# Post-norm Mamba-like block with FP4 feed-forward: skip, silus, copies and g product moved up, scales interleaved, loop written out

## The reference

```
xp, z  = split(x @ W_in)                           # W_in 256 x 1024
xc     = silu(causal conv over time(xp, 4 taps) + conv_b)
ssm    = xc @ W_xproj                              # 33 columns: delta, B (16), C (16)
delta  = softplus(ssm[..., 0])
h_mean = einsum(xc, delta * B) / L                 # one 512 x 16 state per batch
y      = (einsum(h_mean, C) + D * xc) * silu(z)
x      = layernorm(x + y @ W_out)
gate, up = fq(x) @ fq(w_gate).T, fq(x) @ fq(w_up).T   # 704 columns each
h      = silu(gate) * up
x      = layernorm(x + fq(h) @ fq(w_down).T)
```

## Time and profile before

| | before |
|---|---|
| median of 3 timed runs | 2334.24 us (2331.59 to 2337.22) |
| profiled execution | 2339.92 us, span 2338.1 us |
| mean granted clock of TensorE | 0.959 |
| busy: PE, PEld, DVE, ACT, POOL | 2050.8, 1615.6, 1701.5, 1279.5, 988.0 us |
| DMA | 191.35 MB, mean 82 GB/s |

### The profile page before, as it was taken

The page is one execution under the profiler, slowest core; times in us unless marked ns, Lnnn a source line. Parts: engine busy times, 40 slices in busy tenths (PEclk is TensorE's granted clock), DMA queues, the critical chain, the costliest instruction groups (busy, mean ns, idle before and its releaser), DMA issues.

```text
span 2338.1 us, 38729 instructions
## 1 busy us (share of the span) xinstructions
PE 2050.8 (88%) x10532; PEld 1615.6 (69%) x10532; DVE 1701.5 (73%) x3292; ACT 1279.5 (55%) x2612; POOL 988.0 (42%) x1643
## 2 busy tenths in 40 slices
PE   2887799999899998999999999899989999888886
PEld 1555577777777777777777777777767777666665
DVE  6223477877787777777777787878778877777775
ACT  2556555655555656555655565555555655433343
POOL 2222344444444444444444444444444444434342
PEclk9879999999999999999999999999999999888898
DMA  2223322222222222222222222222222222111100
GB/s 74 86 72 113 111 93 95 84 86 83 94 85 83 92 96 86 78 88 95 84 92 85 95 84 86 82 87 92 93 83 83 97 84 86 52 57 55 57 30 14
DMA packets 132401, 191.35 MB, mean 82 GB/s; under 512 B 15024, under 2 KB 66096, under 8 KB 132144
## 3 DMA queue, kind: packets, MB, share of 16 engines
q1 hardware_dynamic: 132144, 188.42, 24.4%
HBM read 104.48 MB, written 83.89 MB: 81 GB/s over the span
## 4 chain that ended last, share of the span: by engine, by line
DVE 35%; PE 35%; issue 17%; ACT 10%; DVEq 1%; POOL 1%; SPq 0%; ACTq 0%; DMA 0%; POOLq 0%
PE pgu L483 9%; PE pd L483 7%; PE pc L557 5%; DVE acc L866 5%; DVE hbuf L802 4%; PE pb L483 4%; DVE g L946 4%; DVE hbuf L929 4%; PE pa L483 3%; ACT hbuf L717 2%; DVE hbuf L808 2%; DVE qsx L795 2%; PE pc L569 2%; DVE qsh L795 2%; DVE hqT L938 2%
## 5 line engine op out<-in xcount | busy, mean ns | idle before, releaser
L483 PE MATMUL pgu<-wgu_hi,xqT 128*128 128x512 f32 (+1 forms) x1536 | 437.8, 394 | 3.5 <-ACT xqT L762 1.7
L483 PE MATMUL pd<-wd_hi,hqT 128*128 128x256 f32 (+1 forms) x1536 | 344.9, 306 | 32.6 <-DVE r L959 28.2
L675 ACT ACTIVATE dev<-r,sum 128x256 f32<-128x256 f32 x256 | 130.1, 508 | 405.4 <-DVE r L959 253.9
L427 POOL TENSOR_TENSOR hq<-hnq,qsh 128x704 f32<-128x704 bf16 x128 | 177.7, 1388 | 378.9 <-DVE hnq L811 378.9
L483 PEld LDWEIGHTS pgu<-wgu_hi,xqT 128*128 128x128 f32 x1536 | 286.7, 194 | 68.5 <-issue 6.0
L483 PEld LDWEIGHTS pd<-wd_hi,hqT 128*128 128x128 f32 (+1 forms) x1536 | 267.3, 198 | 59.0 <-issue 38.8
L546 PE MATMUL pd<-wout,g 128*128 128x256 f32 x1024 | 254.8, 392 | 0.0
L483 PE MATMUL pgu<-wgu_lo,xqT 128*128 128x512 f32 (+1 forms) x768 | 233.8, 386 | 0.0
L483 PE MATMUL pd<-wd_lo,hqT 128*128 128x256 f32 (+1 forms) x768 | 224.7, 293 | 0.0
L414 POOL TENSOR_TENSOR acc<-acc,tap 128x512 f32<-128x512 f32 x128 | 163.0, 1274 | 133.9 <-ACT tap L740 133.9
L866 DVE SCALAR_TENSOR_TENSOR acc<-xps,cw,acc 128x512 f32<-128x512 f32 x256 | 195.0, 762 | 33.2 <-POOL acc L414 28.7
(11 more groups left out here) (132 smaller groups left out, 4545.0 us busy)
## 6 DMA issues: line engine op xcount, KB each, us to landing
sz_hbm<-szs SPq DMA_DIRECT2D x128, 256.0 KB, 2.1
xc_hbm<-xcs SPq DMA_DIRECT2D x128, 256.0 KB, 2.0
xl<-xc_hbm SPq DMA_DIRECT2D x128, 256.0 KB, 2.8
zl<-sz_hbm SPq DMA_DIRECT2D x128, 256.0 KB, 3.0
xin<-in_L_attn_x_dram SPq DMA_DIRECT2D x32, 512.0 KB, 4.4
xres<-in_L_attn_x_dram SPq DMA_DIRECT2D x128, 128.0 KB, 2.3
out_dram<-outb SPq DMA_DIRECT2D x128, 128.0 KB, 1.7
scratch<-in_L_attn_W_in_dram SPq DMA_DIRECT2D x1, 1024.0 KB, 7.2
```

Source lines behind the costliest of these rows:

```text
L427: pool.tensor_tensor(blocks(hq[:, 0:FF]), blocks(hnq[:, :]), spread(qsh[:, 1, :]), ALU.mult).then_inc(hprod_done, 1)
L483: mm = pe.matmul(bank, lhsT, rhs, start=(m == 0), stop=(m == len(pairs) - 1))
L675: act.activation(dev[:, :], r, ACT.Square, bias=total[:, :], scale=-1.0 * DM, accum_out=ssq[:, :]).then_inc(ssq_done, 1)
```

## The change

Four kinds of edit:
- DVE: the skip L946 moves from behind the remainders of hqT to right behind h = silu(gate) * up (L929), so ahead of h's absmax.
- ACT: the gate's silu goes ahead of the conv's silu; the copies xct (steps 0, 2 and 3) and xqT go ahead of dev and the second Abs.
- POOL: g times silu(z) goes ahead of acc + tap.
- `qsx` and `qsh` are laid out with the three numbers of a block side by side, so absmax, scale and inverse have a step of three words; and `walk` has no loop: all 39 groups are straight code on every engine, with constants as awaited values.

```diff
-        qsx = sb("qsx", [P, 3, QX])
+        qsx = sb("qsx", [P, QX, 3])
-        qsh = sb("qsh", [P, 3, QH])
+        qsh = sb("qsh", [P, QH, 3])
...
-        def walk(body, fori, last=0):
-
-            for g in range(2 * SPS):
-                body(g, g % SPS, g // SPS)
-            with fori(2, B - last) as b:
-                for s in range(SPS):
-                    body(b * SPS + s, s, b)
-            for g in range(NSUP - last * SPS, NSUP + LAG + 2):
+        def walk(body):
+
+            for g in range(NSUP + LAG + 2):
                 body(g, g % SPS, g // SPS)
...
@@ POOL @@
-                        pool.tensor_tensor(blocks(xv[:, :]), blocks(xnq[:, :]), spread(qsx[:, 1, :]),
+                        pool.tensor_tensor(blocks(xv[:, :]), blocks(xnq[:, :]), spread(qsx[:, :, 1]),
                                            ALU.mult).then_inc(xprod_done, 1)
                     if p1:
                         wait_apart(pool, (hist_set, u + 1), (xp_copied, u + 1))
                         pool.tensor_copy(hist[:, j, :], xps[:, ST:ST + KC - 1])
-                        wait_apart(pool, (first_tap, u + 1))
-                        pool.tensor_tensor(acc[:, :], acc[:, :], tap0[:, :], ALU.add).then_inc(tap_done, 1)
                     if p2:
                         pool.wait_ge(yd_done, w + 1)
...
                                            ALU.mult).then_inc(g_ready, 1)
+                    if p1:
+                        wait_apart(pool, (first_tap, u + 1))
+                        pool.tensor_tensor(acc[:, :], acc[:, :], tap0[:, :], ALU.add).then_inc(tap_done, 1)
...
-                                           spread(qsh[:, 1, :]), ALU.mult).then_inc(hprod_done, 1)
+                                           spread(qsh[:, :, 1]), ALU.mult).then_inc(hprod_done, 1)
...
@@ ACT @@
+                    if exists(tg):
+                        act.wait_ge(gu_pe, tg + 1)
+                        at_least(act, hq_link, 6 * tg)
+                        act.activation(hbuf[:, 0:FF], pgu[:, 0:FF], ACT.Silu).then_inc(sg_ready, 1)
                     if exists(v):
                         act.wait_ge(conv, 2 * v + 2)
...
                         act.activation(xcs[:, jb % 2, :], acc[:, :], ACT.Silu).then_inc(xc_ready, 1)
-                    if exists(tg):
-                        act.wait_ge(gu_pe, tg + 1)
-                        at_least(act, hq_link, 6 * tg)
-                        act.activation(hbuf[:, 0:FF], pgu[:, 0:FF], ACT.Silu).then_inc(sg_ready, 1)
...
+                    if j != 1 and exists(v):
+                        act.wait_ge(xct_pe, v + 1)
+                        act.activation(xct[:, :, jb * P:(jb + 1) * P],
+                                       pa[:, :].rearrange("p (t n) -> p t n", t=TPS), ACT.Copy)\
+                            .then_inc(xct_copied, 1)
+                    if exists(tx):
+                        act.wait_ge(xq_pe, tx + 1)
+                        act.activation(xqT[:, 0:KM, :], pe_[:, 0:DM].rearrange("p (c n) -> p c n", c=KM), ACT.Copy)\
+                            .then_inc(xqT_hi, 1)
                     if exists(to):
                         deviations(r_done, to, r1[:, j, :], sum1, ssq1, ssq1_done)
...
@@ DVE @@
-            small_x = [qsx[:, r, :] for r in range(3)]
-            small_h = [qsh[:, r, :] for r in range(3)]
+            small_x = [qsx[:, :, r] for r in range(3)]
+            small_h = [qsh[:, :, r] for r in range(3)]
...
                         dve.tensor_tensor(h, h_big, pgu[:, FF:2 * FF], ALU.mult).then_inc(h_done, 1)
+                    if p2:
+                        dve.wait_ge(y_pe, w + 1)
+                        dve.wait_ge(xl_landed[j % 2], 16 * (2 * i + j // 2 + 1))
+                        at_least(dve, o_pe, 4 * i - 4)
+                        dve.scalar_tensor_tensor(g[:, second(s) % 2, j, :], xl[:, j % 2, :], dsk[:, j:j + 1], pc[:, :],
+                                                 ALU.mult, ALU.add).then_inc(yd_done, 1)
+                    if exists(tg):
                         dve.wait_ge(h_done, tg + 1)
                         q_absmax(h, small_h).then_inc(hq_link, 1)
...
```

28 lines of the change are left out of this document (11 added, 17 removed).

## The result

| | before | after |
|---|---|---|
| median of 4 timed runs | 2335.73 us (2331.59 to 2339.78) | 2148.99 us (2146.92 to 2151.27) |
| profiled execution | 2339.92 us, span 2338.1 us | 2148.43 us, span 2146.6 us |
| mean granted clock of TensorE | 0.959 | 0.974 |

The ratio is 0.9201, with a 95% interval of 0.9181 to 0.922: 187 us or 8% less. The forecast was 2184 us, with 2160 to 2215 as its own range and 2140 to 2250 with two rivals taken in. It had the sign and the place; the kernel is 35 us faster than that, inside the wide range and 11 us under the narrow one.

The account below looks back on a forecast made before the run. PE, 88% busy, was taken to bound the kernel, idle mainly waiting for DVE's g and ACT's xct. Waits 100, fill 8, edges and batch ends 38, tail 4 make 150: 2184 us median, own range 2160 to 2215, with rivals 2140 to 2250.

Parts of the forecast that it names:

- two rivals: Rival A (2240 us, chance 0.2) and rival B (2155 us, chance 0.08), taken in for the range 2140 to 2250.
- rival B: In the tail, PE's clock returns from 0.87 to 1.00: 29 us less, time 2155; chance 0.08.
- signs that were named: Profile after: no PE waits for g or xct, middle group 60.7 to 61.5 us, PE over 95% busy, no edge waits.
- the slack that was worked out: On DVE, g would end at 7.7 us of the step where PE needs it at 8.51: 0.8 us or more.
- xct's 0.73 us: On PE, the C transposes' wait for ACT's xct copy, in a group's last step, goes with the copy moved ahead.
- Rival A: Behind each removed PE wait a shorter one shows, or DVE becomes the bound; time about 2240, chance 0.2.
- rival C: On DVE, interleaving does not free L795 from waiting beside POOL; same time as forecast, inside its 0.67 chance.
- rival D: On DVE, strided scales are slow to read or write; 2413 us at 2.5 times the duration; chance 0.03.
- 24 x 4.18 = 100 us: In the middle's 24 groups, PE's 4.18 us idle per group goes: 100 us gained.
- Edges and batch ends: Five loop edges at 4.6 us go whole; six batch ends keep 1 us each: 38 us gained.
- The fill: In the two full groups' worth of steps ahead of the loop, PE idle 21.8 us: 8 us gained.
- The tail: From 1982 us on, a ring that keeps its length but for 0.2 us of silu waiting in 20 steps: 4 us.

Follow-up runs that it names:

- Three kernels: Before, 2336 to 2338 us; after with DVE's skip back behind the remainders, 2234.67 us; after with ACT's copies back behind dev and the second Abs, 2220.41 us.
- the second profile of after: The kernel after, unchanged, run once more: 2147.00 us, 0.9176 of before.
- one worth 3 us by its idle time: The kernel after with DVE's first residual r moved ahead of h's scale and inverse: 2120.97 us against 2147.00 for after.

## Why the prediction was right, and where it was short

The time lies in the stated range, and the mechanism of the middle (waits for g and xct gone, edges gone, POOL's order and scales worth nothing) is the one forecast. The number itself is partly luck: the forecast's own range, 2160 to 2215, was missed, and 2149 lies in the stated one only because that was widened down to 2140 for rival B, whose mechanism gave 11 of its 29 us. Two terms were too small, the floor of PE and the tail. Of the signs that were named, all came but one: a middle group is 59.67 us and not 60.7 to 61.5.

**The skip.** Right, in the mechanism: g is done 0.98 us ahead of L565, with the slack that was worked out (0.8 or more), DVE now waits for y, and taking this part out costs 86 us.

**Silu.** Right that PE does not need it in an ordinary group. It is worth 10 us, 7.6 of them in the middle, at batch ends, where I had left 1 us for a late g whatever ACT does. In the tail, where the forecast gave it all of its 4 us, it is worth nothing: `xbig` stands ahead of the gate's silu in both orders, and with the silu back a full-clock step is 11.7 us as in after.

**Copies.** The step counted xct's 0.73 us as a term of its own beside the waits for g. The sum holds for the whole change, but the terms are not independent: without the copies the same place waits 2.0 to 2.3 us. Rival A (a new wait behind each one removed) is what the kernel with the skip alone shows in kind, though the wait left is longer than before and for xct, which rival A did not name; what keeps it from the kernel after is the copies. Had only the skip been proposed, this working would have promised over 100 us for 46.

**POOL's order, scales.** Nothing, as said; rival C holds, and rival D has no price: DVE's absmax and divide of h take 0.88 and 0.89 us after as before.

**The sum, term by term.** The 24 groups were put at 24 x 4.18 = 100 us; they gave 24 x (64.90 - 59.67) = 125.5. The idle time was right and the floor was wrong. The forecast took PE's busy time in before, 60.73 a group, as what PE needs, and that includes about 0.2 us for each of five restarts behind a wait: this is the term that the sum lacked. Three kernels agree on it: five waits 1.06 us, four 0.79, one 0.24. The spans differ by 191.5 and not by 150, and 25.5 of these 41.5 us are this. Edges and batch ends: 38 forecast (23 and 15), 160.5 - 125.5 = 35 measured, of which the groups with an edge are 18.4, so the edges were put too high and the batch ends about right; a batch end still costs 1.4 us (61.31 + 59.41 - 2 x 59.67), where I left 1. The fill: 8 forecast, 12 measured, and 8.1 against the second profile of after (151.5), so nothing can be said of it.

**The tail: 4 forecast, 20 measured.** Here a step failed: that the same DVE instructions stand in the tail in another order, "so it keeps its length". They do not take the same time in another order. In a step of before DVE has a divide of 1.33 us, beside POOL's g product, and a wait for ACT's xqT:

```profile
2125.96 1.33 DVE L802 SCALAR_TENSOR_TENSOR hbuf<-hbuf,qsh 128x704 f32<-128x704 f32 x1
2128.43 0.43 DVE L974 TENSOR_TENSOR xqT<-pe_,xqT 128x256 fp32r<-128x256 f32 x1 [1.13 <-ACT xqT L762]
```

and in a step of after:

```profile
1967.79 0.89 DVE L798 SCALAR_TENSOR_TENSOR hbuf<-hbuf,qsh 128x704 f32<-128x704 f32 x1
1968.60 0.42 DVE L971 TENSOR_TENSOR xqT<-pe_,xqT 128x256 fp32r<-128x256 f32 x1
```

The skip alone takes the divide to 0.89, the copies alone take the wait for xqT, and either brings a full-clock step from 12.43 to 11.86, both to 11.70. That is 19 x 0.73 = 14 us if every step ran at full clock. But many do not: before, every other step of the later tail is 14.83. As measured, 9.2 of the 20 us are idle time of PE (40.88 and 31.63) and 10.8 busy time (225.5 and 214.7), at a clock of 0.87 and 0.91. Rival B's time, 2155, is nearer than the forecast's own, but its mechanism gave 11 us of the 29 it was priced at. The 41.5 us are 25.5 of floor, 16 of tail and 4.2 of fill, less 3 at edges and batch ends and 1.3 at start and end.

**Loop.** Right in the main: 17 us in the full kernel and 29 alone for the 23 forecast. A group with an edge lost 3.7 us alone and 3.8 in the full kernel, for the 4.6 forecast; the stretch at half clock was there at four edges of five in before and at two of five with the loop put back. The last batch, from which the forecast took a batch end at 3.5 us, had one of the shorter ones.

## What to carry to other kernels

Before pricing a removed wait, move every consumer behind it up by the same amount and ask again which one is late next: here the wait for g and the wait for xct were one slack seen at two places, and alone the two edits gave 34 and 43 us of the 141 that they gave together in the middle. Take the floor of PE from a stretch in which it never waits, since its busy time beside waits contains their restarts. Where a stretch stands at mixed clocks, a small edit can shift it between the levels: one worth 3 us by its idle time gave 26 here, which no sum would have told; leave room for it in the range. And read the length of a disturbance, such as a loop edge, group by group before dividing a total by their number.
